# Self-attention: GpSimd subtracts the maximum from four heads at once, and ScalarE takes one exponential of 512 columns

## The reference

```
q = (hidden_states @ Wq).reshape(b, s, NUM_HEADS, HEAD_DIM)
kv = hidden_states @ Wkv
k, v = (kv[..., :HEAD_DIM], kv[..., HEAD_DIM:])
scores = jnp.einsum('bqhd,bkd->bhqk', q, k) * scale
bias = slopes[:, None, None] * (pos[None, None, :] - pos[None, :, None]).astype(jnp.float32)
scores = jnp.where(causal[None, None], scores + bias[None], -jnp.inf)
attn = jax.nn.softmax(scores, axis=-1)
out = jnp.einsum('bhqk,bkd->bqhd', attn, v).reshape(b, s, h)
return out @ Wo
...
x = x + _L0_attn_ref(_layernorm(x, axis=-1), L0_attn_Wq, L0_attn_Wkv, L0_attn_Wo)
x = x + _L0_xattn_ref(_layernorm(x, axis=-1), ctx_4096, ctx_4096, pos_BxS2, mask_BxSxS2_ik0, ...)
x = x + _L0_ffn_ref(_layernorm(x, axis=-1), L0_ffn_W_gate, L0_ffn_W_up, L0_ffn_W_down)
```

## Time and profile before

| what | value |
|---|---|
| time, median of 2 runs | 1013.69 us (1013.65 to 1013.73) |
| the profiled execution's own time | 1013.56 us |
| its span in the profile | 1011.7 us |
| TensorE busy in the span | 983.9 us (97%) |
| VectorE | 592.7 us (59%) |
| ScalarE | 429.5 us (42%) |
| GpSimd | 381.9 us (38%) |

### The profile page before, as it was taken

One profiled execution on the slowest core, in us unless ns is written; L12 is line 12 of the kernel. 1 busy time (PEld: TensorE's weight loads), 2 busy tenths in 40 slices (PEclk: granted clock), 3 DMA queues, 4 the chain that ended last, 5 costly groups with the idle time before them and its releaser, 6 DMA issues. The chain is left out here.

```text
span 1011.7 us, 15673 instructions
## 1 busy us (share of the span) xinstructions
PE 983.9 (97%) x5096; PEld 806.0 (80%) x5096; DVE 592.7 (59%) x973; ACT 429.5 (42%) x1239; POOL 381.9 (38%) x375
## 2 busy tenths in 40 slices
PE   5999999989999999999999999999999989999998
PEld 3777777877888888888888888888888768888787
DVE  3766666636776676666766657667666873343100
ACT  2777777751532533533533433533432543333100
POOL 6422222253652642642642633634523422222200
PEclk8999999989999999999999999999999999999999
DMA  6000000211120210210210210200200112222001
GB/s 202 13 11 11 11 10 10 63 52 52 41 61 5 63 43 0 73 31 0 73 31 0 73 31 0 81 23 13 80 0 1 33 32 70 65 71 67 11 32 42
DMA packets 49954, 39.98 MB, mean 40 GB/s; under 512 B 4128, under 2 KB 40096, under 8 KB 49920
## 3 DMA queue, kind: packets, MB, share of 16 engines
q1 hardware_dynamic: 49536, 38.48, 12.9%
q0 software_dynamic: 384, 1.05, 0.4%
HBM read 37.43 MB, written 2.10 MB: 39 GB/s over the span
## 5 line engine op out<-in xcount | busy, mean ns | idle before, releaser
L617 PE MATMUL bank<-cross_wo_hl,cross_outT_hl 128*128 128x512 f32 x768 | 191.7, 398 | 1.0 <-POOL cross_wo_hl L611 0.6
L617 PE MATMUL bank<-hsT_hl,cross_wqkv_hl 128*128 128x512 f32 x768 | 188.2, 394 | 0.0
L617 PEld LDWEIGHTS bank<-cross_wo_hl,cross_outT_hl 128*128 128x128 f32 x768 | 143.1, 188 | 35.5 <-POOL cross_wo_hl L611 1.6
L617 PEld LDWEIGHTS bank<-hsT_hl,cross_wqkv_hl 128*128 128x128 f32 x768 | 141.9, 188 | 29.3
L932 ACT ACTIVATE cross_scores<-cross_scores,cross_negmax 128x128 f32<-128x128 f32 x256 | 99.8, 391 | 127.2 <-DVE cross_negmax L870 127.2
L792 POOL TENSOR_TENSOR cross_qT<-rotated,rotated_other_half 128x512 f32<-128x512 f32 x64 | 82.8, 1293 | 161.9 <-DVE rotated_other_half L834 161.9
L617 PE MATMUL bank<-hsT_hl,ff_gate_upT_hl 128*128 128x512 f32 (+1 forms) x528 | 120.4, 390 | 2.7 <-DVE ff_gate_upT_hl L1134 2.7
L617 PEld LDWEIGHTS bank<-hsT_hl,ff_gate_upT_hl 128*128 128x128 f32 (+1 forms) x528 | 97.7, 185 | 25.0 <-DVE ff_gate_upT_hl L1134 3.1
L942 ACT CAST cross_outT_hl<-bank 128x512 fp32r<-128x512 f32 x64 | 37.1, 580 | 143.4 <-PE bank L617 142.5
L832 DVE TENSOR_TENSOR rotated<-bank,cosT 128x512 f32<-128x512 f32 x80 | 55.2, 691 | 71.3 <-PE bank L617 71.1
L617 PE MATMUL bank<-ctxT_hl,cross_wqkv_hl 128*128 128x512 f32 x384 | 94.3, 394 | 1.1 <-PEq L74 1.1
(11 more groups left out here) (115 smaller groups left out, 1534.9 us busy)
## 6 DMA issues: line engine op xcount, KB each, us to landing
staged_rows<-in_wq SPq DMA_DIRECT2D x32, 256.0 KB, 2.9
staged_rows<-in_wo SPq DMA_DIRECT2D x32, 256.0 KB, 2.7
staged_rows<-in_wg SPq DMA_DIRECT2D x10, 256.0 KB, 2.9
staged_rows<-in_wu SPq DMA_DIRECT2D x10, 256.0 KB, 2.9
staged_rows<-in_wd SPq DMA_DIRECT2D x10, 256.0 KB, 2.8
ctx_tok<-in_ctx SPq DMA_DIRECT2D x8, 256.0 KB, 2.6
staged_rows<-in_wk SPq DMA_DIRECT2D x8, 256.0 KB, 3.1
staged_rows<-in_wv SPq DMA_DIRECT2D x8, 256.0 KB, 3.1
```

The lines of the kernel that those rows point to most:

```text
L617: i = nc.tensor.matmul(out, stationary[:, a], moving[:, b], start=(first and k == 0), stop=(last and k == 2))
```

## The change

The exponential no longer takes the maximum as its bias. GpSimd adds the negated maximum to all four heads in `S`, in place (`subtract_max`, which waits for `max1`), and signals a new semaphore `shifted1`; ScalarE waits for that and takes one exponential of 128x512. GpSimd's other work of a sequence is placed between the subtractions: `xn_of` to step 1, `hs_of` to step 2, `keys_by_head` to step 6, and in sequence 0 the subtractions stand between the pieces of the bias.

```
--- before.py
+++ after.py
@@ -183,25 +183,35 @@
                                                 head_of_row[:].unsqueeze(2).to_broadcast([P, QUAD, P]), ALU.mult)
                 i.then_inc(sem["kexp"], 1)
 
+            def subtract_max(n, s):
+                pool.wait_ge(sem["max1"], n + 1)
+                nc.gpsimd.tensor_tensor(S[:, s % 2], S[:, s % 2], negmax[:, s % 2, :].unsqueeze(2).to_broadcast([P, QUAD, P]), ALU.add).then_inc(sem["shifted1"], 1)
+
             pool.wait_ge(sem["exponent_ready"], 2)
             rstd_of_x(0, 1)
             pool.wait_ge(sem["rel_loaded"], 16)
             for h in range(HEADS):
                 nc.gpsimd.tensor_scalar(bias[:, h, :], rel[:], slopes[h], None, ALU.mult).then_inc(sem["bias"], 1)
-                if h == 15:
+                if h == 7:
                     pool.wait_ge(sem["head_of_row_loaded"], 16)
                     keys_by_head(0)
+                if h == 11:
                     rstd_of_x(1, 2)
                     xn_of(1)
+                if h >= 11 and h % QUAD == QUAD - 1:
+                    subtract_max(h // QUAD - 2, h // QUAD - 2)
 
             def body(b):
 
-                if not since(b, SEQS - 1) and since(b, 1):
-                    xn_of(b + 1)
-                if since(b, 2) and not since(b, SEQS):
-                    hs_of(b - 2)
-                if not since(b, SEQS - 1):
-                    keys_by_head(b + 1)
+                for s in range(STEPS):
+                    if s == 1 and not since(b, SEQS - 1) and since(b, 1):
+                        xn_of(b + 1)
+                    if s == 2 and since(b, 2) and not since(b, SEQS):
+                        hs_of(b - 2)
+                    if s == 6 and not since(b, SEQS - 1):
+                        keys_by_head(b + 1)
+                    if (since(b, 1) or s >= STEPS - 2) and not since(b, SEQS):
+                        subtract_max(STEPS * b + s, s)
 
             body(0)
             rstd_of_x(2, SEQS)
@@ -392,12 +402,10 @@
                     if s == 1 and front:
                         copy_xnT(b + 1)
                     if scores:
-                        act.wait_ge(sem["max1"], n + 1)
+                        act.wait_ge(sem["shifted1"], n + 1)
                         if since(b, 1) or s >= 2:
                             act.wait_ge(sem["probs_transposed1"], n - 1)
-                        for j in range(QUAD):
-                            e = nc.scalar.activation(PR[:, s % 2, j, :], S[:, s % 2, j, :], ACT.Exp, bias=negmax[:, s % 2, j:j + 1])
-                        e.then_inc(sem["exp1"], 1)
+                        nc.scalar.activation(PR[:, s % 2], S[:, s % 2], ACT.Exp).then_inc(sem["exp1"], 1)
                     if s == 7 and front and since(b, 1):
                         copy_qT(b + 1, 0)
                     if s == 3 and front:
@@ -1250,7 +1258,7 @@
 
 SEMAPHORES = """x_first rel_loaded head_of_row_loaded wkv1_loaded wq1_loaded x_rest pos_loaded wo1_loaded mask_loaded
 ctx_loaded ident_zero ident_ready exponent_ready ones_ready mv0 mv1 var_eps0 var_eps1 rstd0 rstd1
-kv_high kv_copied scores1 kexp bias tables_loaded stats0 stats1 xn_transposed xn_centred hs_centred xn wk8 mask_is_set exp1 biased1 max1 ctx_high
+kv_high kv_copied scores1 kexp bias tables_loaded stats0 stats1 xn_transposed xn_centred hs_centred xn wk8 mask_is_set exp1 shifted1 biased1 max1 ctx_high
 ctx_low pv1 rsum1 attn_transposed attn out1 x1 hs_transposed hs hs_high hs_low kv1 xnT q1 q_transposed q_high q_copied qT
 probs_transposed1 probsT1 attnT tables_transposed out_stored
 piece_split piece_high rope_read roped rinv2 probs2 projected out2
```

## The result

The changed kernel takes 1066.32 us (median of 2 runs, 1066.31 to 1066.32) against 1013.69 before: 1.0519 times as long, 95% interval 1.0500 to 1.0538. The profiled execution took 1066.31 with a span of 1064.5, which is 52.8 more than before.

The account below looks back on a forecast made before the run. The prediction took TensorE to bound the self-attention. Five terms, 6.0 + 11.2 + 6.6 + 15.7 + 3.4 = 42.9 us on 1013.6, gave 1056.5 us (chance 0.67), with a range from 1036 to 1080.

Parts of the forecast that it names:

- Sequence 0: First term: subtractions between GpSimd's bias pieces make sequence 1 start at 47.4 instead of 41.39, +6.0 us.
- The head of the sequences: Sequences 1 to 6: xn queued behind the first subtraction makes TensorE wait 1.87 us each, +11.2 us.
- The end of the sequences: Third term, sequences 1 to 6: qT copied behind the later last exponential, 1.1 us each, +6.6 us (3.0 to 10.2).
- The case in which VectorE is held for one more instruction: Sequence ends: GpSimd's back-to-back keys and subtraction 6 hold VectorE's last maximum another 1.04 us; 1.5 with the hop.
- The end of the self-attention: Fourth term, after sequence 7: gathers wait behind the subtractions, delaying the chain to TensorE, +15.7 us.
- The clock: Fifth term: TensorE's waits for xn bring one fall to half clock, +3.4 us (none to six falls).
- the clock falls in every sequence: First rival: the new waits bring six clock falls, 20.4 us instead of 3.4, giving 1073.5; chance 0.17.
- the first gather: Sign of being right: after sequence 7 it starts some 40 us later than 202 by the profile's own time.
- the rival of the hidden waits: "The waits hide each other": sequence ends cost nothing, sequences 0 and 7 their least; 26 us, 1040; chance 0.13.
- the second term: Head of sequences 1 to 6: TensorE waits 1.87 us each for xn behind the first subtraction, +11.2 us.
- between them TensorE has long work at once: Argument against a clock fall in every sequence: TensorE works long between the new waits.
- Not slower: Rival: shorter exponentials reach ScalarE's users sooner, TensorE regains some 9 us of waits, 1005; chance 0.03.

Follow-up runs that it names:

- tail_only: Changed kernel with only sequence 7's end relaid on GpSimd: two gathers before the first subtraction, first piece_low behind subtraction 3, other gathers behind subtractions 4 to 7; 1044.6 us.
- qT_ahead: three_moves, plus ScalarE copying qT ahead of a sequence's last exponential instead of behind it; 1024.0 us.
- before_xn_late: Kernel before, with GpSimd in sequences 1 to 6 waiting for the first maximum and doing one idle pass before normalising xn; 1027.7 us.
- qT_ahead_alone: Changed kernel with one move: ScalarE copies qT ahead of a sequence's last exponential, xn staying behind the first subtraction; 1054.5 us.
- xn_first: Changed kernel with GpSimd normalising xn ahead of the first subtraction in sequences 1 to 6; 1045.2, 1046.2, 1052.1 and 1052.9 us.
- three_moves: Changed kernel with xn ahead of the first subtraction, one gather behind each subtraction of sequence 7, and sequence 0 as before; 1030.2 us.
- gathers_between: Changed kernel with one gather behind each of sequence 7's eight subtractions, instead of all eight behind the last; 1059.3 us.
- seq0_as_before: Changed kernel with sequence 0 in its old order: no GpSimd subtraction there and ScalarE's old four exponentials; 1054.1 us.
- best_order: qT_ahead with sequence 7 relaid on GpSimd: two gathers before the first subtraction, first piece_low behind subtraction 3, other gathers behind later subtractions; 1013.7 us.

## Why the prediction was right

The time lies 9.8 us above the forecast of 1056.5, at the upper edge of what its terms allow (1066) and inside its range. Two terms hit, two were too large and one was much too small.

- **Sequence 0** was priced 6.0 and cost 7.3, by the mechanism named. Undoing it alone brings the start of sequence 1 back to 40.55.
- **The head of the sequences** was priced 6 x 1.87 = 11.2; it cost 5 x 1.5 = 7.5. Sequence 1 has no such wait, since TensorE ran at half the clock there and came late itself.
- **The end of the sequences** was priced 6.6 and cost 4.1: in the list of waits up to 275 us seven for `qT` make 5.6, of which 1.5 belong to sequence 0. That is 0.7 a sequence, near the hop's 0.5, the low end. The case in which VectorE is held for one more instruction did not come; GpSimd was held instead (below).
- **The end of the self-attention** was priced 15.7 and cost 15.6, gathers 14.6 later for the 14.7 worked out. tail_only removes all of it.
- **The clock** was the step that failed: "I count one such fall: **+3.4**". Each of sequences 1 to 6 had a stretch at half, and these cost 16.7 (half of 33.4 us). Waits of 11.6 and clock of 16.7 make 28.3 of the 28.5 us of these sequences.

So the forecast held in part by luck: 6 us too much in waits stood against 13 too little in clock. In the clock its first rival, "the clock falls in every sequence", was right, and the time lies nearer to that rival (1073.5) than to the forecast. Of the signs, the subtraction at 1.04, the exponential at 0.63 and TensorE's wait of 14.33 at the end came; the waits for `xn` were 1.5 instead of 1.9 and missing in sequence 1, the first gather came 50 us later instead of 40, and the stretch behind the self-attention grew by 1.4. Of the signs of being wrong, the clock at half came in every sequence, though through under a fifth of their time and not most of it. Two slips in the working changed little: by its own rows exponential 2 ends 2.35 later and not 2.2, and the rival of the hidden waits has 6 x 1.7 where the second term's 1.87 belongs, 1.0 us.

The argument against the first rival, "between them TensorE has long work at once", held in 9 of 10 sequences where the wait for `xn` is alone, and failed in 15 of 20 where a wait for `qT` ends some 4 us ahead of it (106.04 and 110.18 in sequence 3). The four cells, in falls over the five sequences 2 to 6, each from the one profiled execution of its kernel:

| | no wait for `xn` | wait for `xn` |
|---|---|---|
| no wait for `qT` | 0 (before), 0 (qT_ahead) | 0 (before_xn_late), 1 (qT_ahead_alone) |
| wait for `qT` | 0 (xn_first), 0 (three_moves) | 5 (changed kernel), 5 (gathers_between), 3 (seq0_as_before), 2 (tail_only) |

The Trainium skill (TensorE: Matmul & The Clock Gate, section "What's actually happening") states that the clock is low by default and that activity releases it. The trace agrees in kind, since the falls stand behind waits. But in sequences 2 to 6 a wait of 1.4 to 1.8 us by itself brought one fall in ten, and tail_only shows that equal waits need not have equal falls. The table is a count over few executions, and the clock of two runs of xn_first, which have no trace, may not fit its cell. That pairs of waits bring falls more often is what these profiles show; what picks the sequence that falls stays open.

"Not slower" fell as argued: the subtraction costs 1.04 to 1.49 us, and even without any subtraction the gain is 0.3%. "The waits hide each other" fell too, as three_moves shows places that add.

## What to carry to other kernels

Before moving work to an engine with room, list what else is in its queue at that place and who needs that next: here the average load of GpSimd rose to only 42%, and the waits came from one instruction standing ahead of another. The order could be mended (GpSimd was idle for 3.9 us right ahead of the first subtraction, and best_order is as fast as the kernel before), but a change that relieves an engine off the critical path paid next to nothing even then. Two short waits of the engine that sets the pace within some microseconds of each other can cost more through the clock than through themselves, or less (in sequences 2 to 6, 13.6 us against 11.1 in the changed kernel and 6.8 against 11.1 in tail_only), so price the clock where waits come in pairs, and give it a wide range.

## What the runs showed of the hardware

GpSimd's subtraction took 1.49 us instead of 1.04 at 45.52, and likewise in step 6 of sequences 1 to 6, where it follows the keys while VectorE's subtraction of two SBUF tiles (line 324, 1.34 us instead of 0.69) is under way:

```profile
44.77 1.34 DVE L324 TENSOR_TENSOR ctxT_hl<-ctx_tok,ctxT_hl 128x512 fp32r<-128x512 f32 x1 [0.17 <-ACT ctxT_hl L421]
```

The Trainium skill (SBUF — State Buffer, section "SBUF: two separate sides") states that the two exclude each other for a whole instruction; the trace agrees for both sides, in that VectorE ended 0.55 us behind the keys and the subtraction behind them 0.90 us behind VectorE. And a wait of 1.47 us for `hs` in three_moves, with one of 0.33 some 2 us ahead of it, was followed by 17 us at half the clock, though TensorE was busy 16.7 of 18 us there; qT_ahead, with the same two waits in sequence 7 and none for `qT` ahead of them, shows the same fall.
